# Attention and experts for 16 images: side work packed into earlier slots, scores issued one slot ahead late in each phase, and a shorter chain from the maxima

## The reference, cut to what matters

```python
q = (x @ Wq).reshape(b, n, h, dh).transpose(0, 2, 1, 3)      # h = 8 heads, dh = 16; k, v alike
dots = jnp.einsum('bhnd,bhmd->bhnm', q, k) * SCALE
top_dots, top_inds = jax.lax.top_k(dots, TOPK)               # TOPK = 32
attn = jax.nn.softmax(top_dots, axis=-1)
out = jnp.einsum('bhnk,bhnkd->bhnd', attn, vg)               # vg: the rows of v at top_inds
...
t = t + _L1_attn_ref(_ln_t(t), L1_attn_Wq, L1_attn_Wk, L1_attn_Wv, L1_attn_Wo, L1_attn_bo)
t = t + _L1_ffn_ref(_ln_t(t), L1_ffn_gate_w, L1_ffn_thr_w, L1_ffn_fc1_w, L1_ffn_lora_A, L1_ffn_lora_B, L1_ffn_fc2_w)
```

## Time and profile before

| | |
|---|---|
| median of 3 runs | 9082.76 us (9075.89 to 9084.97) |
| profiled execution, its own time | 9074.8 us |
| its span | 9073.1 us |
| attention and experts, from the first score to the last phase | 4815 to 9016 us of the span |
| one image of it (turn to turn, 6355.77 to 6618.10) | 262.3 us |
| PE busy in the whole span | 87% |
| DVE busy, ACT busy | 59%, 42% |

### The profile page before, as it was taken

One profiled execution on the slowest core, in us unless ns is written; L12 is line 12 of the kernel. 1 busy time (PEld: TensorE's weight loads), 2 busy tenths in 40 slices (PEclk: granted clock), 3 DMA queues, 4 the chain that ended last, 5 costly groups with the idle time before them and its releaser, 6 DMA issues. The chain is left out here.

```text
span 9073.1 us, 601301 instructions
## 1 busy us (share of the span) xinstructions
PE 7923.9 (87%) x265196; PEld 4270.7 (47%) x265196; DVE 5380.0 (59%) x15117; ACT 3778.8 (42%) x7262; POOL 1947.5 (21%) x2028
## 2 busy tenths in 40 slices
PE   3999999999999778668856999999999999999998
PEld 2677777777777666557741222222222222222222
DVE  4677777777777546643324555555555555555553
ACT  3455555555555334324422333333334333333333
POOL 1455555555555334300000000000000000000000
PEclk9999999999999889779967999999999999999999
DMA  0000000000000000000010000000000000000000
GB/s 37 1 0 0 0 0 0 0 0 0 0 0 0 0 0 0 1 1 0 0 42 14 15 17 17 12 16 15 13 17 15 17 15 12 17 10 17 15 17 5
DMA packets 58886, 82.10 MB, mean 9 GB/s; under 512 B 26101, under 2 KB 27706, under 8 KB 58426
## 3 DMA queue, kind: packets, MB, share of 16 engines
q1 hardware_dynamic: 58426, 76.45, 3.2%
HBM read 17.63 MB, written 8.39 MB: 3 GB/s over the span
## 5 line engine op out<-in xcount | busy, mean ns | idle before, releaser
L1867 DVE MAX8 w_best<-psum 128x8 f32<-128x128 f32 x8192 | 1725.0, 283 | 1301.9 <-PE psum L1409 1300.5
L1850 ACT ACTIVATE w_exp<-psum 128x512 f32<-128x512 f32 x2048 | 1220.1, 596 | 2291.7 <-PE psum L1418 2289.4
L1428 PE MATMUL psum<-w_exp,w_v 128*32 128x512 f32 x4096 | 2087.6, 608 | 3.0 <-ACT w_inverse L1461 2.7
L1409 PE MATMUL psum<-w_k,w_q 96*128 96x512 bf16 x2048 | 637.3, 394 | 239.7 <-DMA w_k<-w_parts 145.0
L1418 PE MATMUL psum<-w_q,w_k 99*128 99x512 bf16 x2048 | 798.2, 390 | 1.4 <-ACT w_q L1443 1.4
L499 PE MATMUL psum<-e_prod_u,e_j 32*32 32x64 f32 x49152 | 769.8, 215 | 30.5 <-ACT e_prod_u L579 25.1
L499 PEld LDWEIGHTS psum<-e_prod_u,e_j 32*32 32x32 f32 x49152 | 708.0, 105 | 183.2 <-issue 183.2
L1409 PEld LDWEIGHTS psum<-w_k,w_q 96*128 96x128 bf16 x2048 | 123.7, 98 | 1071.4 <-issue 1071.2
L1428 PEld LDWEIGHTS psum<-w_exp,w_v 128*32 128x32 f32 x4096 | 276.0, 108 | 716.8 <-issue 716.8
L653 POOL TENSOR_TENSOR e_diag<-odd,e_eye 128x512 f32<-128x512 f32 x384 | 488.0, 1271 | 559.4 <-PE psum L473 521.3
L547 ACT ACTIVATE e_square<-e_off 128x512 bf16<-128x512 f32 x384 | 242.1, 630 | 844.0 <-POOL e_off L657 844.0
(11 more groups left out here) (268 smaller groups left out, 10889.3 us busy)
## 6 DMA issues: line engine op xcount, KB each, us to landing
w_q<-w_parts SPq DMA_DIRECT2D x768, 32.0 KB, 2.0
w_k<-w_parts SPq DMA_DIRECT2D x768, 32.0 KB, 2.0
odd<-in_x SPq DMA_DIRECT2D x1, 8192.0 KB, 23.1
even<-in_x SPq DMA_DIRECT2D x1, 8192.0 KB, 23.2
out<-w_t SPq DMA_DIRECT2D x16, 512.0 KB, 2.6
w_hid<-in_fc SPq DMA_DIRECT2D x2, 256.0 KB
w_wo<-in_wo SPq DMA_DIRECT2D x8, 8.0 KB
w_wq<-in_wq SPq DMA_DIRECT2D x1, 64.0 KB
```

What stands on the lines that cost most here:

```text
L1409: last = nc.tensor.matmul(banks[base + k], w.q[0:DEPTH, 4 * g + j, q0:q0 + P], w.k[0:DEPTH, 4 * g + j, half(k)], start=True, stop=True)
L1428: nc.tensor.matmul(banks[7][slot(j), :], w.v[:, kt, 4 * g + j, :], w.exp[x % 4][:], start=(kt == 0), stop=(kt == KT - 1)).then_inc(s.weigh ...
L1850: nc.scalar.activation(w.exp[x % 4][:], banks[4 + x % 2], ACT.Exp).then_inc(s.exp_done, 1)
L1867: last = nc.vector.max(w.best[:, i, o, :], banks[o // 4][:, P * (o % 4):P * (o % 4) + P])
```

## The change

Three things. First, the slot numbers of the side work: the back work starts in slot 1 of phase 1 in place of slot 2 and ends in slot 5 of phase 2 in place of slot 9 (all eight hidden products lie now in slots 8 to 15 of phase 1), and the front work takes slots 7 to 15 of phase 2; only the values, `second_parts_act` for k and `third_parts_dve` for k are left in slots 0 and 1 of phase 3. Second, from slot 8 on the scores of slot i + 1 are issued in the middle of slot i, just behind its side work, and before the second transposed score of the slot. Third, `maxima_dve` has one step less between the maxima and the last part.

```diff
+    SPRINT = 8
...
     def maxima_dve(dve, at):
-        k = Count(s.maxima, at * 12)
+        k = Count(s.maxima, at * 11)
...
-        chained(dve, k, nc.vector.tensor_scalar(rest[:, 0], w.top[:], -1.0, None, ALU.mult))
-        chained(dve, k, nc.vector.tensor_copy(part[:, :, 0], rest[:, 0]))
-        chained(dve, k, nc.vector.tensor_tensor(rest[:, 1], rest[:, 0], part[:, :, 0], ALU.subtract))
+        chained(dve, k, nc.vector.tensor_scalar(part[:, :, 0], w.top[:], -1.0, None, ALU.mult))
+        chained(dve, k, nc.vector.scalar_tensor_tensor(rest[:, 1], w.top[:], -1.0, part[:, :, 0], ALU.mult, ALU.subtract))
...
         if phase == 2 and front:
-            if i == 11:
+            if i == 7:
...
-            elif i == 13:
+            elif i == 9:
                 variances_pe(pe, n_front)
-        if phase == 3 and front:
-            if i == 0:
+            elif i == 11:
                 spread_pe(pe, n_front)
-            elif i == 2:
+            elif i == 12:
                 project_pe(pe, ahead, 0, n_front)
-            elif i == 4:
+            elif i == 14:
                 project_pe(pe, ahead, 1, n_front)
-            elif i == 5:
-                values_pe(EXTRA, 0)
+        if phase == 3 and front and i == 0:
+            values_pe(EXTRA, 0)
...
-            if scored:
+            if scored and i <= SPRINT:
                 if i >= 1:
                     hold(pe, s.read_max, at * 16 + i)
                 score_pe(phase, i, 0)
...
                 if x % 2 == 0 and i >= 1 and scored:
                     beside_pe(pe, b, phase, i, back, front)
+                    if SPRINT <= i < 15:
+                        hold(pe, s.read_max, at * 16 + (i + 1))
+                        score_pe(phase, i + 1, 0)
```

More of the change, by code:

```diff
@@ L1675, in beside_pe @@
             if back:
-                if i == 2:
+                if i == 1:
                     hold(pe, s.v_out, b * 2 + 2)
                     join_pe(pe, behind, 0)
+                elif i == 2:
+                    join_pe(pe, behind, 1)
                 elif i == 3:
-                    join_pe(pe, behind, 1)
-                elif i == 5:
                     hold(pe, s.residual, behind * 2 + 2)
                     average_pe(n_back, w.t)
+                elif i == 5:
+                    variances_pe(pe, n_back)
                 elif i == 7:
-                    variances_pe(pe, n_back)
-                elif i == 10:
                     spread_pe(pe, n_back)
-                elif i == 12:
+                elif i == 8:
                     gates_pe(pe, behind, n_back)
-                if i >= 12:
-                    hidden_pe(pe, behind, i - 12)
+                if i >= 8:
+                    hidden_pe(pe, behind, i - 8)
         if phase == 2 and back:
             if i < 4:
-                hidden_pe(pe, behind, i + 4)
-            elif i < 8:
                 for e in (2 * (i % 2), 2 * (i % 2) + 1):
-                    low_pe(pe, behind, (i - 4) // 2, e)
-            elif i == 8:
+                    low_pe(pe, behind, i // 2, e)
+            elif i == 4:
                 gates_turned_pe(pe, behind)
-            elif i == 9:
+            elif i == 5:
                 expert_out_pe(pe, behind)
         if phase == 2 and front:
-            if i == 11:
+            if i == 7:
                 if back:
@@ L1727, in beside_act @@
             if back:
-                if i == 6:
+                if i == 4:
                     squares_act(act, n_back)
+                elif i == 6:
+                    root_act(act, n_back)
                 elif i == 8:
-                    root_act(act, n_back)
-                elif i == 12:
                     gate_exp_act(act, behind)
-                if i == 12 or i == 14:
-                    hidden_act(act, behind, i - 12)
+                if i >= 8 and i % 2 == 0:
+                    hidden_act(act, behind, i - 8)
         if phase == 2 and back:
[L1737 to L1740, removed]
+            if i == 1 or i == 3:
+                low_act(act, behind, i // 2)
         if phase == 2 and front:
-            if i == 12:
+            if i == 8:
                 squares_act(act, n_front)
-            elif i == 14:
+            elif i == 10:
                 root_act(act, n_front)
+            elif i == 12 or i == 14:
+                first_parts_act(act, ahead, (i - 12) // 2)
+            elif i == 13:
+                second_parts_act(act, ahead, 0)
         if phase == 3 and front:
[L1747 to L1751, removed]
+            if i == 0:
                 values_act(act, ahead, EXTRA, 0)
+                second_parts_act(act, ahead, 1)
     def beside_dve(dve, b, phase, i, back, front):
@@ L1757, in beside_dve @@
         if phase == 1 and back:
-            if i == 2 or i == 3:
-                join_dve(dve, behind, i - 2)
+            if i == 1 or i == 2:
+                join_dve(dve, behind, i - 1)
+            elif i == 3:
+                centred_dve(dve, n_back, w.t)
             elif i == 5:
-                centred_dve(dve, n_back, w.t)
+                variance_dve(dve, n_back)
+            elif i == 6:
+                root_dve(dve, n_back)
             elif i == 7:
-                variance_dve(dve, n_back)
+                normal_dve(dve, n_back)
@@ L1764, in beside_dve @@
             elif i == 8:
[L1765 to L1768, removed]
                 logits_dve(dve, behind)
-            elif i == 13 or i == 15:
-                hidden_dve(dve, behind, i - 12)
+            elif i >= 9 and i % 2 == 1:
+                hidden_dve(dve, behind, i - 8)
         if phase == 2 and back:
-            if i == 1 or i == 3:
-                hidden_dve(dve, behind, i + 4)
+            if i == 0:
+                softmax_dve(dve, behind)
+            elif i == 2:
+                weights_dve(dve, behind)
@@ L1775, in beside_dve @@
             elif i == 4:
[L1776 to L1779, removed]
                 mix_dve(dve, behind)
-            elif i == 9:
+            elif i == 5:
                 finish_dve(dve, behind)
         if phase == 2 and front:
-            if i == 11:
+            if i == 7:
                 centred_dve(dve, n_front, tokens(ahead))
+            elif i == 9:
+                variance_dve(dve, n_front)
+            elif i == 10:
+                root_dve(dve, n_front)
+            elif i == 11:
+                normal_dve(dve, n_front)
+            elif i == 12 or i == 14:
+                first_rests_dve(dve, ahead, (i - 12) // 2)
@@ L1786, in beside_dve @@
             elif i == 13:
-                variance_dve(dve, n_front)
-            elif i == 14:
-                root_dve(dve, n_front)
+                third_parts_dve(dve, ahead, 0)
         if phase == 3 and front:
[L1791 to L1796, removed]
+            if i == 1:
+                third_parts_dve(dve, ahead, 1)
```

## The result

The changed kernel takes 9065.8 us (median of 10 runs, 9050.0 to 9081.7), the kernel before 9084.7 (10 runs): ratio 0.9979, 95% interval 0.9969 to 0.9988. I had forecast 8975 us, 108 less. It is faster by 19 us, which is hardly more than the 18 us that I had called no change. The profiled execution has a span of 9055.7 us, 17.4 less than before.

What follows compares the result with a forecast made beforehand. PE, busy nearly always, was taken as the bound, with waits for copies (145.0 us) and maxima (117.3). A, C, D, E over 15 images (-86.2) and B over 31 phases (-21.7) give -108: 9082.8 to 8975 us, range 8930 to 9025.

Steps and rivals of the forecast that it cites:

- term A: Start of phase 0: earlier row copies end PE's wait and the slow clock behind it, -7.57 us in each of 15 images.
- D: Phase 2, packed with front work: early scores delay ACT's side work, +3.53 us per image, bounds 0.4 and 6.
- B, quiet phases: Phases 0 and 3: the 1.54 us wait at the end goes, slot 8 gains 0.84; net -0.70 in 31 phases.
- C, phase 1: Phase 1: 0.33 us saved at its end and a shorter wait at the spread, together -0.57 us per image.
- E: Phase 3: side work leaves its first slots, and with it waits of 0.97 and 0.17 us: -1.14 us per image.
- Rival 1, the clock: New short PE idles halve the clock: 9103 us, slower, chance 0.05; one to three stretches, 9010 to 9050, chance 0.13.
- Rivals 2 to 4: Phase 2 costs little, 8928 us (chance 0.12); copies wait as before, 9089 (0.03); packing costs more, 9012 to 9050 (0.05).
- rival 4: Packing in phase 2 costs more than the upper bound of 6 us per image: 9012 to 9050 us, chance 0.05.
- The sign for MAX8: PE's waits for MAX8 in the attention were to grow by some 45 us.

Runs made afterwards that it cites:

- unroll_all: The changed kernel with the loop over images 1 to 14 written out on all engines but SP: 8988.4 us, ratio 0.9896 to the kernel before.
- fill_turn: unroll_all with matmuls whose result nobody reads in two waits of phase 2, ahead of slot 14's scores and the turn: 8967.1 us, ratio 0.9887.
- no_sprint: The changed kernel without early scores, all at the head of their slot: 8975.6 us, ratio 0.9891 to the kernel before.
- no_sprint_2: The changed kernel with early scores in phases 0, 1 and 3 only, none in phase 2: 8961.5 us, ratio 0.9879 to the kernel before.
- before_unroll: The kernel before with its loop over the images written out on all engines but SP: 9053.0 us, ratio 0.9967 to the kernel before.

## Why the prediction was wrong

The sum said -108 us. From the first turn to the last the attention took 4099.1 us before, and 4085.3 after: -14. With the loop written out it is 4007.1 (-92), and with two waits of phase 2 filled as well 3989.8 (-109). The windows from first to last turn of before, after and unroll_all (the first busy time is PE's) tell where the missing 94 us are:

```profile
4867.00:8967.00 4100.00, 3807.93 (x12045) 1031.13 (x12046) 2359.13 (x9775) 1591.56 (x2815) 0.00 (x0) 0.98 0.06 14
4868.00:8954.00 4086.00, 3843.03 (x12046) 1042.61 (x12045) 2344.63 (x9711) 1587.83 (x2815) 0.00 (x0) 0.97 0.06 15
4873.00:8881.00 4008.00, 3807.49 (x12047) 1037.77 (x12046) 2344.42 (x9711) 1585.30 (x2815) 0.00 (x0) 0.98 0.06 15
```

| us, against before | PE idle | PE busy, the same matmuls |
|---|---|---|
| forecast (22 of the 108 are the slow clock won back, 15 x 1.47) | -86 | -22 |
| after | -49 | +35 |
| unroll_all | -92 | 0 |

So the loop's return takes 78 us, 43 of standing still and 35 of slower matmuls behind it. The idle time without it is what the sum said, and 6 us better. The other 22 us are again slower matmuls: the clock that was to be won back at the start of phase 0 falls elsewhere, in phase 2 and at the start of phase 3. That fill_turn comes out at -109 is therefore partly luck; it still has 78 us at half clock.

Two steps failed. The first, and the larger, is in term A: "What is late next: the scores of slot 0 wait for ACT's copy of the turned maxima, 3.27 us behind the turn". The second is the clock: the 1.47 us that A counts as won, and nothing put down for it in D.

- **A, the copies.** Right in what it removes: they begin 11.2 us behind the turn of phase 2 (forecast 10) and are waited for no more. Wrong in what is late next. I took the 3.27 us from the start of a phase 2, where the code runs straight on, and carried it to a phase 0, where the loop returns. The wait of 7.43 us had covered the returns of PE and of DVE. What is late next is DVE's first MAX8. The late scores of slot 0 and the late MAX8s cost 3.7 us at each of 13 returns, and there are 1.6 of slow clock behind them; unroll_all wins 75 us.
- **B, quiet phases.** Right, if a little less. No wait at the turns of phases 0 and 3, 0.79 in slot 8 (forecast 0.84). Phase 3 at its shortest is 52.7 with early scores and 53.0 without (no_sprint).
- **C, phase 1.** Right: 1.29 at the turn, 0.22 at the spread (forecast 1.28, 0.27).
- **D, phase 2.** The waits are where they were put: 0.79 in slot 8, 0.65 at the spread (0.82), 1.91 ahead of the scores of slot 14 (2.08), 2.33 at the turn (2.45), and none for the third parts of q (0.2). That makes +2.8 where the sum had 3.53. Of the clock the sum took nothing here, and phase 2 takes 76.3 us where it doesn't fall and 78.3 on average: the 2 us between them are the clock.
- **E.** Right: the waits of 0.97 and 0.17 us are gone from phase 3.
- **Rival 1, the clock.** I gave it 0.18 in all, and had rejected it by the turns of 1.54 and 1.61 us. The slow stretches from the second turn on are 171 us before and 201 after. Of those of before 116 us lay at the starts of phase 0, where PE was idle for most of their time; now 61 do, and those elsewhere went from 55 to 140 us, which is 1.7 more stretches of 3.4 us per image. They lie on busy time. The rule of the Trainium skill that spoke against the change (TensorE: Matmul & The Clock Gate, section "A second HAM failure mode: psum-queue depth-cycling") says that short idles between groups of matmuls let the engine swing to its lower clock. The trace agrees for the waits of 1.91 and 2.33 us in phase 2, with 0.91 over the phase 3 behind them and 1.00 with these filled. But the time lies near this rival's (9103) by luck more than by this: of the 94 us missing 43 are the engines' standing still at the return, which it doesn't name.
- **Rivals 2 to 4.** Phase 2 did not come cheap, and the copies did not wait. Its waits stayed within the bounds of D, so rival 4 didn't come either. The early scores should have been weighed by phase: they earn some 0.3 us in a quiet phase (phase 3 is 52.7 us in no_sprint_2 and 53.0 in no_sprint) and cost 4.4 us (78.3 - 73.9) in phase 2.
- **The sign for MAX8.** I wrote that its waits grow by some 45 us; the terms named there add up to 49, so 136 us were to be expected and not 132. Measured are 162.6, and what is above lies in slot 1 of phase 0, behind the return (36.0 us in the changed kernel, 9.3 in unroll_all). Two more slips bear on nothing: by the cases the chances are 0.92 for faster and 0.03 for the same, and the copies begin 36.6 us behind the turn, not 36.4.

## What to carry to other kernels

When a long wait goes, look at everything that happens while it lasts, on each engine, and not only at the next semaphore: here the return of the loop lay under a wait for a DMA, and took back 5.2 of the 7.6 us that this wait and the slow clock behind it were to give. Compare the place with one that has the same code around it. Issuing the next scores earlier on PE makes everything behind them later for the engines that wait for PE's results: it pays where these have nothing else to do, and costs where side work hangs on them. And count what PE does slowly as well as what it waits for: here idle time fell by 49 us, and 35 of them went into slower matmuls.

## What the runs showed of the hardware

- The return of this loop (14 images, some 870 instructions per pass on DVE) makes DVE stand still for 3.22 us and 0.60 more a few instructions on, where it stands 0.35 us in unroll_all; its first MAX8 comes 2.9 us later behind the turn (medians 6.90 and 4.01). PE stands still for 2.68 us where it would for 1.36. Seven transfers of instructions, 72 KB, go with each return. Written out, the changed kernel is not slower in any phase.
- SP's slow issues go with transfers of instructions: in before, where a copy is issued in 0.63 us, three of the 48 take 1.2 to 1.5, and each of the 39 such issues in images 1 to 13 lies within 0.3 us of the start of a transfer of 16 KB. before_unroll has ten.
- Weighted sums of neighbouring heads write different groups of 32 partitions, and two of them in a row take the time of one in the records (x4 in 1.05 us). The waits at the turns were forecast with that, and came out.
- In phase 2 of unroll_all, PE idles for 1.91 us ahead of the scores of slot 14 and for 2.33 ahead of the turn, and the granted clock is at half at the start of phase 3 in 13 of 15 images; with these waits filled with matmuls that do nothing, in none. The matmuls behind them then run in full: phase 3 is 52.6 us on average in place of 54.1.
